# Layer 1's gate rows inside the attention's ring, key stacks of 48 rows, and transfers dealt to other queues

## The chip, the cores and the metric

The kernel runs on one core of a Trainium2 chip. The metric is the device time of one execution in microseconds (us), lower is better. Engines: TensorE (PE, its weight loads PEld), VectorE (DVE), ScalarE (ACT), GpSimd (POOL), and SyncE (SP), which only issues transfers; ScalarE issues transfers too, on a queue of its own.

## The reference

Two layers on 2 x 1024 tokens of 128 channels. Each layer computes an attention `s` and a feed-forward result `g` of the same normalised input; layer 1's feed-forward part has an expert-weighted attention of its own.

```python
def _layernorm(x, eps=1e-05): ...            # (x - mean) / sqrt(var + eps), per token
# x: 2 x 1024 tokens x 128
xn = _layernorm(x)                            # layer 0
s = _L0_attn_ref(xn, ...)                     # 16 heads of 8, bias by position, softmax over 1024 keys
g = _silu(_L0_ffn_ref(xn, ...))               # router, 8 experts of 256, 2 shared
x = x + s * g
xn = _layernorm(x)                            # layer 1
s = _L1_attn_ref(xn, W_Q, W_K, W_V, W_O)      # 16 heads of 8, causal softmax
g = _silu(_L1_ffn_ref(xn, ...))               # see below
x = x + s * g

def _gating(flat_hs, sim, gates, min_experts):
    logits = _normalize(flat_hs, -1) @ _normalize(sim, 0) - sigmoid(gates)
    ...                                       # relu, at least two experts kept, softmax over them

def _L1_ffn_ref(x, ...):
    n1 = _layernorm(x, ln1_w, ln1_b)
    rw = _gating(n1, smha_sim, smha_gates, 2)
    q = einsum('btc,ech,bte->bth', n1, q_proj, rw)   # k and v alike
    hs = x + (causal attention of q, k, v, put back by o_proj and rw)
    n2 = _layernorm(hs, ln2_w, ln2_b)
    rw2 = _gating(n2, moe_sim, moe_gates, 2)
    return hs + (8 experts w1, gelu, w2, weighted by rw2)
```

## The kernel before

Everything is written out by hand: each engine has one program, and semaphores join them. Layer 0's feed-forward part and its attention come first; then, in `attention(1)`, layer 1's attention; then layer 1's expert part, whose first expert units already run in the attention's last two halves.

**Halves and steps.** The heads of a batch are taken in groups of four (HG = 4). A group's 1024 queries are two halves, so there are 16 halves H (HALVES). For each half the kernel computes the transposed scores, key tile by key tile ("T steps": 4 in an even half, 8 in an odd one, with 512, 384, 256 and 128 queries in the last four), takes their exponentials on ScalarE (line 1090), and multiplies by the values one step later (`av_step`). The exponent needs each row's maximum. It comes from a second product of the same scores with the queries on the partitions ("S units", `ring_unit` and `both`), whose results pass through four PSUM banks, the ring; VectorE reduces each (line 1605). When all S units of a half are reduced, unit "K" combines them (line 1598), GpSimd splits the maxima in three bf16 parts (`max_parts`, lines 916 to 919), unit "M" transposes the parts on TensorE, VectorE copies them to `mrow` (line 1610), and SP's `max_rows` (line 689) puts them as rows 48 to 50 under the half's query stack with four transfers. TensorE starts half H after all of them have landed (`pe.wait_ge(A["m_ld"], 64 * (H + 1))`). The key stack has ones in rows 48 to 50, so one product of 51 rows subtracts the maximum. These ones stand in DRAM with the keys, and `load_group` fetches 51 rows (TROWS) of keys and 48 (ROWS) of queries per piece.

**The order.** `s_stream` gives the order of units; `stands_before` puts 16 S units of half 0, K and M of half 0, and 14 S units of half 1 ahead of the first half; `even_steps` deals the rest to the T steps: (8, 8, 8, 10) S units to the four steps of half 0, four to every later step until none are left. TensorE issues an S unit right behind each T product. VectorE follows the same order.

**Around layer 1's start.** Before the 16 first S units VectorE does `normal_again(1)` (line 1379) and `batch_values(1)` (line 1741) for the second batch. TensorE transposes `zz` in four chunks; ScalarE makes `n1T` and its square. Behind the 14 S units, `gate_rows` (lines 1835, 1888) computes the gate logits and sums of squares in banks 4 to 6; ScalarE copies the rows (line 1050), VectorE the logits (`gate_raw`, lines 1486 to 1488), ScalarE takes a root (line 1118) and then loads its table for the exponential.

**SP's loop.** For half H: `sums_out(H - 1)` (line 693) fetches the softmax sums; `sums_back(H - 1)` stores their inverse (line 699) and loads it back spread (line 704); `max_rows(H + 2)`; then what the table `then` says: in 9 to 13 the gate weights as rows spread over 128 partitions (`rw_behind`, line 819, 1 MB each). VectorE's `invert(H - 1)` (line 1620) waits for the sums behind step 3 of an even half and step 4 of an odd one. ScalarE issues the loads of the next key and query stacks, and of projection weights, at the start of halves 1 to 9 (lines 601, 604).

Of the kernel before, what the change touches and what calls it, by code (L numbers as in the profile page):

```python
# [33 lines left out]
P = 128  # L34
# [136 lines left out]
def even_steps(stream, first):  # L171
# [116 lines left out]
def block_net(nc, a, out):  # L288
    ctx = ExitStack()
    with ctx:  # L290
# [11 lines left out]
        k_dram = [dram(f"k_dram{l}", (GROUPS * HG, TROWS, SEQ), BF16) for l in range(2)]  # L302
# [76 lines left out]
        ones_rows = bf(62, 2)[0:32 * PARTS, :]  # L379
# [212 lines left out]
        def load_group(eng, l, G, pieces=range(4)):  # L592


            for piece in pieces:
                hh = piece // 2
                dr, rows, at_ = ((q_dram[l], ROWS, q_at[l]), (k_dram[l], TROWS, k_at[l]))[piece % 2]
                src = bass.AP(tensor=dr.tensor, offset=(G * HG + hh) * rows * SEQ,
                              ap=[[SEQ, rows], [2 * rows * SEQ, PAIRS], [1, SEQ]])
                dst = bf(at_[G], 4)[64 * hh:64 * hh + rows, :].rearrange("p (r t) -> p r t", r=PAIRS)  # L600
                eng.dma_start(dst, src).then_inc(att[l][f"ld{G // 2}"], 16)

# [4 lines left out]
        def store_qk(eng, l, b):  # L607
# [15 lines left out]
            for row, parts in K_ROWS:  # L623
                for n in range(parts):
                    dst = bass.AP(tensor=k_dram[l].tensor, offset=(b * HEADS * TROWS + (row + n) * HD) * SEQ,
                                  ap=[[TROWS * SEQ, HEADS], [SEQ, HD], [1, SEQ]])
# [7 lines left out]
        def _(sp):  # L634
# [45 lines left out]
            def max_rows(l, H):  # L680

                A, G, h = att[l], H // 2, H % 2
                sp.wait_ge(A["ring_free"], place[l]["M", H] + 1)
                if H:
                    sp.wait_ge(A["m_ld"], 64 * H)
                for j in range(HG):
                    row, first = 64 * (j % 2) + ROWS, 12 * (PAIRS * (j % 2) + j // 2)
                    dst = Qs[l][G][row:row + PARTS, j // 2, 512 * h:512 * (h + 1)].rearrange("p (q t) -> p q t", t=P)
                    sp.dma_start(dst, mrow[first:first + 12, H % 2, :]).then_inc(A["m_ld"], 16)  # L689
# [16 lines left out]
            def attention_feed(l, then):  # L706
# [4 lines left out]
                store_qk(sp, 1, 1)  # L711
                max_rows(l, 1)
# [66 lines left out]
            for l in range(2):  # L779
# [1674 lines left out]
```

## Time and profile before

| | us |
|---|---|
| median of 3 runs | 1192.28 (1189.81 to 1196.51) |
| the profiled execution | 1190.6, of which its span is 1188.8 |
| busy in the span: PE, DVE, ACT, POOL | 1063.3, 811.4, 646.5, 210.0 |
| layer 1's attention, first S unit to its last M | about 639 to 897 |
| mean granted TensorE clock | 0.941 of full speed |

Times in the rows are us from the span's start. The page gives for each engine the busy time and its share; a timeline row gives start, duration, engine, line, operation, "output<-input", a count where alike instructions are merged, and in brackets how long the engine had been idle and what released it.

### The profile page before, as it was taken

To read this page: it belongs to the slowest core of one execution; us is meant where nothing else is said; L and a number is where in the kernel's file an instruction comes from. 1 tells how busy PE (TensorE), PEld (TensorE's weight loads), DVE (VectorE), ACT (ScalarE), POOL (GpSimd) and SP (SyncE) were. 2 spreads that over 40 slices of the span, in tenths; PEclk is the share of its full clock that TensorE was granted. 3 is DMA by queue.
4 is the path that set the end of the run, shared out by engine and by line. 5 is a ranking of instruction groups with operands and counts; after the bars stand their busy time and mean duration, and the time that the engine had idled before them with its cause. 6 is when DMAs were issued, how large, how long until landed. Compare 5 with 4: busy or idle time off the path is not lost.

```text
span 1188.8 us, 19388 instructions
## 1 busy us (share of the span) xinstructions
PE 1063.3 (89%) x7308; PEld 490.5 (41%) x7308; DVE 811.4 (68%) x1625; ACT 646.5 (54%) x1259; POOL 210.0 (18%) x327
## 2 busy tenths in 40 slices
PE   5699999999999999999977888899889999888767
PEld 4455555552222222222234333334334468543444
DVE  7656666667887888875377778888674156655654
ACT  4522222226898888889733366677565432442534
POOL 2244554510010101010003011113221000001100
PEclk9899999999999999999976799899898999999888
DMA  4684112001010111000023422211322020000431
GB/s 128 201 229 140 50 66 81 2 1 28 25 43 30 43 30 34 12 20 20 11 66 97 151 66 75 60 45 42 126 86 88 10 80 1 1 1 0 143 143 36
DMA packets 57398, 74.63 MB, mean 63 GB/s; under 512 B 15720, under 2 KB 35032, under 8 KB 55512
## 3 DMA queue, kind: packets, MB, share of 16 engines
q1 hardware_dynamic: 48516, 62.13, 16.5%
q10 hardware_dynamic: 8788, 11.26, 3.4%
q8 instruction: 58, 0.95, 0.3%
q14 instruction: 36, 0.29, 0.1%
HBM read 58.18 MB, written 14.54 MB: 61 GB/s over the span
## 4 chain that ended last, share of the span: by engine, by line
PE 69%; DVE 19%; ACT 6%; issue 3%; DMA 2%; SPq 1%; ACTq 0%; POOL 0%; DVEq 0%
PE PS L1835 67%; DVE mx L1605 9%; ACT arena L1090 4%; DMA sums<-arena 1%; PE PS L1848 1%; DVE arena L1809 1%; DVE arena L1404 1%; DVE arena L1379 1%; DVE arena L1364 0%; DVE arena L1407 0%; DVE small L1795 0%; SPq L689 0%; DMA arena<-in_L_attn_x 0%; PE PS L2307 0%; DVE fw L1700 0%
## 5 line engine op out<-in xcount | busy, mean ns | idle before, releaser
L1835 PE MATMUL PS<-arena 128*32 128x512 f32 (+10 forms) x3656 | 568.1, 479 | 50.3 <-DVE mx L1605 22.8
L1605 DVE TENSOR_REDUCE mx<-PS 128x1 f32<-128x512 f32 (+3 forms) x896 | 511.9, 625 | 88.7 <-PE PS L1835 86.8
L1090 ACT ACTIVATE arena<-PS 128x512 f32<-128x512 f32 (+3 forms) x896 | 435.3, 558 | 149.3 <-PE PS L1835 145.0
L1835 PEld LDWEIGHTS PS<-arena 128*32 128x32 f32 (+3 forms) x3656 | 149.1, 104 | 409.5 <-ACT arena L1090 183.6
L1835 PE MATMUL PS<-x_hi,w_hi_lo 128*128 128x512 f32 x320 | 145.7, 496 | 6.8 <-ACT fw L1133 2.3
L1133 ACT ACTIVATE fw<-PS 128x512 f32<-128x512 f32 x80 | 47.8, 598 | 168.0 <-PE PS L1835 168.0
L1700 DVE TENSOR_TENSOR fw<-PS,fw 128x512 f32<-128x512 f32 x80 | 55.3, 692 | 79.2 <-PE PS L1835 76.6
L1835 PE MATMUL PS<-fw 128*128 128x512 f32 (+3 forms) x184 | 98.4, 620 | 0.0
L1001 POOL TENSOR_TENSOR fw<-fw,arena 128x512 f32<-128x512 f32 x64 | 81.8, 1280 | 76.1 <-DVE fw L1700 76.1
L925 POOL TENSOR_TENSOR arena<-arena,fw 128x512 f32<-128x512 f32 x31 | 39.4, 1272 | 262.8 <-DMA fw<-sum_dram 262.8
L1835 PEld LDWEIGHTS PS<-x_hi,w_hi_lo 128*128 128x128 f32 x320 | 61.5, 192 | 37.8 <-issue 21.2
L1835 PE MATMUL PS<-arena,fw 128*128 128x512 f32 x128 | 66.1, 635 | 5.2 <-DVE arena L1791 5.2
L1835 PE MATMUL PS<-x_lo,w_hi_lo 128*128 128x512 f32 x160 | 63.8, 399 | 0.0
L1835 PE MATMUL PS<-identb_sw,mask_kq_sw 64*128 64x128 bf16 x256 | 55.2, 230 | 0.0
L1835 PE MATMUL PS<-identb,mask_kq 64*128 64x128 bf16 x256 | 54.4, 229 | 0.0
L1835 PE MATMUL PS<-mask_kq,identb 64*128 64x128 bf16 x256 | 53.5, 223 | 0.0
L1835 PE MATMUL PS<-mask_kq_sw,identb_sw 64*128 64x128 bf16 x256 | 53.4, 223 | 0.0
L916 POOL CAST mparts<-mneg 128x16 bf16<-128x16 f32 x24 | 4.7, 196 | 260.0 <-DVE mneg L1598 260.0
L1835 PE MATMUL PS<-e_hi_lo,w_hi_lo 128*128 128x512 f32 x144 | 45.3, 395 | 0.0
L1835 PE MATMUL PS<-e_hi_lo,fw_lo 128*128 128x512 f32 x104 | 41.5, 400 | 0.0
L1821 DVE TENSOR_TENSOR arena<-arena 128x512 f32<-128x512 f32 x32 | 21.9, 697 | 26.3 <-ACT arena L1321 26.3
L1835 PEld LDWEIGHTS PS<-x_lo,w_hi_lo 128*128 128x128 f32 x160 | 30.9, 193 | 21.6 <-issue 17.9
(317 smaller groups left out, 1110.1 us busy)
## 6 DMA issues: line engine op xcount, KB each, us to landing
arena<-comb_dram SPq DMA_DIRECT2D x14, 1024.0 KB, 4.8
arena<-comb_dram SPq DMA_DIRECT2D x18, 512.0 KB, 7.4
fw<-sum_dram SPq DMA_DIRECT2D x31, 256.0 KB
q_dram<-arena SPq DMA_DIRECT2D x24, 256.0 KB, 3.7
k_dram<-arena SPq DMA_DIRECT2D x24, 256.0 KB, 4.0
arena<-k_dram ACTq DMA_DIRECT2D x20, 204.0 KB
arena<-q_dram ACTq DMA_DIRECT2D x20, 192.0 KB
arena<-drev_dram SPq DMA_DIRECT2D x16, 192.0 KB, 6.9
```

Source lines behind the costliest of these rows:

```text
L925: g.tensor_tensor(OT[:, G, 512 * h:512 * (h + 1)], Osb[:, h, :], RB[l][:, h, :], ALU.mult).then_inc(A["r_done"], 1)
L1001: g.tensor_tensor(fu[:, k % 4, :], fu[:, k % 4, :], cwb[:, (e - 1) % 2, chunk(part_of(k))], ALU.mult).then_inc(g_made, 1)
L1090: s.activation(Pr[:, m % 8, 0:w], st_bank(l, m, 0, w), ACT.Exp).then_inc(A["e_done"], 1)
L1133: s.activation(ft[:, k % 2, :], bank(2), ACT.Silu).then_inc(a_made, 1)
L1379: ins = v.tensor_scalar(dst[:, t, :], src[:, t, :], small[:, 0, t:t + 1], small[:, 2, t:t + 1], ALU.subtract, ALU.mult)
L1404: v.tensor_tensor(src, src, dst[:, 0, :], ALU.subtract).then_inc(rest_done, 1)
L1605: v.reduce_max(mx[:, H % 2, kh, n:n + 1], bank(ring_bank[l][U], 0, w), axis=AX.X, negate=True).then_inc(A["ring_free"], 1)
L1700: v.tensor_tensor(fu[:, k % 4, :], bank(3), ft[:, k % 2, :], ALU.mult).then_inc(u_made, 1)
L1809: v.tensor_tensor(Xo[:, x % 4, :], attnT[:, chunk(n)], rwb[e][:, chunk(n)], ALU.mult).then_inc(ox_made, 1)
L1821: v.tensor_tensor(gg[:, U % 4, :], ga[:, U % 4, :], rwb[e][:, chunk(2 * b + c)], ALU.mult).then_inc(i_g, 1)
L1835: return nc.tensor.matmul(out_, lhsT, rhs, start=start, stop=stop)
L1848: ins = nc.tensor.transpose(bank(first + c, P * k, P * (k + 1)), src(4 * c + k), ident[:, :])
```

## The change

Five things. **Gate rows**: the gate's row product is now a ring unit "R" behind step 1 of half 0 and the transposes with the squares' sum a ring unit "L" behind step 2; VectorE copies both out (the row copy was ScalarE's); the root moves to ScalarE's half 2, step 2, and a one-column exponential is put where it stood. Half 0's steps take (6, 8, 8, 8) S units, four fewer, so that every later unit comes one step later, and the last four S units with K and M of half 15 fall in half 14. **Key stacks**: keys are stored and loaded with 48 rows; the ones go once to `ones_dram` and from there under the stacks, by two transfers at the start and two behind `store_qk(1, 1)`. **First rows**: half 0's four row transfers are issued by SP (two) and ScalarE (two); ScalarE loads group 2 before the `n1T` activations. **Values behind first maxima**: VectorE does `normal_again(1)` behind the first 16 reductions and `batch_values(1)` behind the first `mrow` copy; TensorE transposes two chunks of `zz` before M of half 0 and two behind it. **Weight rows**: the 1 MB weight rows are issued by ScalarE at the start of halves 10 to 13, where SP issued them in loops 9 to 13.

```diff
@@ even_steps: where the score units go
-            count = HG if H else (8, 8, 8, 10)[i]
+            count = HG if H else (6, 8, 8, 8)[i]
...
+        if H == 0:
+            here[1].append(("R",))
+            here[2].append(("L",))
@@ DRAM and ones
-        k_dram = [dram(f"k_dram{l}", (GROUPS * HG, TROWS, SEQ), BF16) for l in range(2)]
+        k_dram = [dram(f"k_dram{l}", (GROUPS * HG, ROWS, SEQ), BF16) for l in range(2)]
+        ones_dram = dram("ones_dram", (8 * PARTS, SEQ), BF16)
...
-        ones_rows = bf(62, 2)[0:32 * PARTS, :]
+        ones_rows = bf(62, 2)[0:8 * PARTS, :]
@@ load_group
-                dr, rows, at_ = ((q_dram[l], ROWS, q_at[l]), (k_dram[l], TROWS, k_at[l]))[piece % 2]
+                dr, at_ = ((q_dram[l], q_at[l]), (k_dram[l], k_at[l]))[piece % 2]
...
+        def send_rows(eng, l, H, heads):
+            A, G, h = att[l], H // 2, H % 2
+            eng.wait_ge(A["ring_free"], place[l]["M", H] + 1)
+            if H:
+                eng.wait_ge(A["m_ld"], 64 * H)
+            for j in heads:
...
+                eng.dma_start(dst, mrow[first:first + 12, H % 2, :]).then_inc(A["m_ld"], 16)
@@ SP
             def max_rows(l, H):
...
+                send_rows(sp, l, H, range(2) if l == 1 and H == 0 else range(HG))
...
                 max_rows(l, 0)
                 store_qk(sp, 1, 1)
+                sp.wait_ge(z_ready, 12)
+                ones_under(32)
                 max_rows(l, 1)
...
-            for l in range(2):
-                dst = bass.AP(tensor=k_dram[l].tensor, offset=ROWS * SEQ, ap=[[TROWS * SEQ, GROUPS * HG], [SEQ, PARTS], [1, SEQ]])
-                sp.dma_start(dst, ones_rows).then_inc(ones_stored, 16)
+            sp.dma_start(ones_dram, ones_rows).then_inc(ones_stored, 16)
+            sp.wait_ge(ones_stored, 16)
+            def ones_under(kib):
+                for hh in range(2):
+                    row = 64 * hh + ROWS
+                    dst = bf(kib, 16)[row:row + PARTS, :].rearrange("p (n t) -> p n t", t=SEQ)
+                    sp.dma_start(dst, ones_dram.rearrange("(p n) t -> p n t", p=PARTS)).then_inc(ones_stored, 16)
+            ones_under(48)
...
-            attention_feed(1, {
-                8: comb_out, 9: lambda: rw_behind(7, 0, 4), 10: lambda: rw_behind(7, 1), 11: lambda: rw_behind(7, 5),
-                12: lambda: rw_behind(11, 2), 13: lambda: rw_behind(11, 3)})
+            attention_feed(1, {8: comb_out})
@@ ScalarE
+                        if l == 1 and H == 2 and i == 2:
+                            root_squares(1)
...
-            act.wait_ge(ones_stored, 16 * 2)
...
+            first_batch()
             for c in range(NC):
                 act.wait_ge(tr_ps, 16 + c + 1)
                 s.activation(n1T[:, 512 * c:512 * (c + 1)], ...).then_inc(tr_ev, 1)
+                if c == 1:
+                    send_rows(act, 1, 0, range(2, HG))
             act.wait_ge(tr_ev, 20)
             s.activation(zz..., n1T[:, :], ACT.Square).then_inc(sq_ready, 1)
-            rows_out(1, 4)
-            root_squares(1)
+            s.activation(gl[:, 1, 159:160], ones[:, 0:1], ACT.Exp)
...
-                -1: first_batch, 1: lambda: next_group(1, 3), 2: later_batch,
+                1: lambda: next_group(1, 3), 2: later_batch,
...
-                HALVES - 2: last_rows})
+                10: lambda: rw_behind(7, 0, 4), 11: lambda: rw_behind(7, 1, 5), 12: lambda: rw_behind(11, 2),
+                13: lambda: rw_behind(11, 3), HALVES - 2: last_rows})
@@ VectorE
-                    sequence(first_units[l])
-                    gate_raw(1)
+                    sequence(first_units[l][:AHEAD])
+                    normal_again(1)
+                    sequence(first_units[l][AHEAD:AHEAD + 2])
+                    batch_values(1)
+                    sequence(first_units[l][AHEAD + 2:])
...
             queries(1)
-            normal_again(1)
-            batch_values(1)
             invert_sums = attention(1)
@@ TensorE
+                    transposes(lambda t: zz[:, t, :], 4, lambda c: pe.wait_ge(z_ready, 7 + c), (0, 1))
+                    for what in first_units[l][AHEAD:AHEAD + 2]:
+                        ring_unit(what)
                     pe.wait_ge(v_ev, 8)
-                    transposes(lambda t: zz[:, t, :], 4, lambda c: pe.wait_ge(z_ready, (7, 8, 11, 12)[c]))
-                    for what in first_units[l][AHEAD:]:
+                    transposes(lambda t: zz[:, t, :], 4, lambda c: pe.wait_ge(z_ready, 9 + c), (2, 3))
+                    for what in first_units[l][AHEAD + 2:]:
                         ring_unit(what)
                     pe.wait_ge(tr_ev, 20)
-                    gate_rows(1, n1T, 4, 6)
-                    pe.wait_ge(ss_ready, 1)
```

VectorE at the start of layer 1's attention, before (mx: maxima, mrow: row copy, gl: gate logits):

```order
L1734 TENSOR_SCALAR arena<-PS 128x512 x2
L1377 RECIPROCAL small<-small 128x8
L1379 TENSOR_SCALAR arena<-arena,small 128x128 x8
L1741 COPY arena<-PS 128x4x4x32 x2
L1605 TENSOR_REDUCE mx<-PS 128x1 x16
L1610 CAST mrow<-PS 48x128
L1605 TENSOR_REDUCE mx<-PS 128x1 x14
L1486 COPY gl<-PS 128x128
L1487 COPY gl<-PS 128x16
L1488 COPY gl<-PS 128x8
```

and in the changed kernel:

```order
L1757 TENSOR_SCALAR arena<-PS 128x512 x2
L1621 TENSOR_REDUCE mx<-PS 128x1 x16
L1394 RECIPROCAL small<-small 128x8
L1396 TENSOR_SCALAR arena<-arena,small 128x128 x8
L1626 CAST mrow<-PS 48x128
L1764 COPY arena<-PS 128x4x4x32 x2
L1621 TENSOR_REDUCE mx<-PS 128x1 x28
L1628 COPY arena<-PS 128x512
L1621 TENSOR_REDUCE mx<-PS 128x1 x5
L1614 TENSOR_TENSOR mneg<-mx 128x16
```

The first 16 reductions now stand ahead of the second batch's normalisation, and the gate copies are gone from behind the 14.

VectorE between the `mrow` copy of half 3 and the inversion of half 1's sums, in half 2, before:

```order
L1598 TENSOR_TENSOR mneg<-mx 128x16
L1605 TENSOR_REDUCE mx<-PS 128x1 x4
L1610 CAST mrow<-PS 48x128
L1605 TENSOR_REDUCE mx<-PS 128x1 x11
L1620 RECIPROCAL rsums<-sums 128x16
```

and in the changed kernel:

```order
L1614 TENSOR_TENSOR mneg<-mx 128x16
L1621 TENSOR_REDUCE mx<-PS 128x1 x4
L1626 CAST mrow<-PS 48x128
L1621 TENSOR_REDUCE mx<-PS 128x1 x7
L1640 RECIPROCAL rsums<-sums 128x16
```

Seven units instead of eleven lie between the copy and the end of the even half; halves 4, 6, 8, 10 and 12 read alike.

## Rows read from the trace of the kernel before

**Rows 1.** The page: the chain that ended last, shares of the span.
```profile
PE 69%; DVE 19%; ACT 6%; issue 3%; DMA 2%; SPq 1%; ACTq 0%; POOL 0%; DVEq 0%
```
**Rows 2.** Timeline of VectorE, layer 1's start.
```profile
636.12 2.14 DVE L1379 TENSOR_SCALAR arena<-arena,small 128x128 f32<-128x128 f32 x8
...
639.39 6.65 DVE L1605 TENSOR_REDUCE mx<-PS 128x1 f32<-128x384 f32 x16
649.01 0.28 DVE L1610 CAST mrow<-PS 48x128 bf16<-48x128 f32 x1 [2.97 <-PE PS L1835]
649.33 6.53 DVE L1605 TENSOR_REDUCE mx<-PS 128x1 f32<-128x512 f32 x14
659.70 0.29 DVE L1486 COPY gl<-PS 128x128 f32<-128x128 f32 x1 [3.83 <-PE PS L1888]
...
660.77 3.61 DVE L1605 TENSOR_REDUCE mx<-PS 128x1 f32<-128x256 f32 x7 [0.63 <-PE PS L1835]
```
**Rows 3.** Timeline of TensorE: zz's transposes, gate rows, half 0, first product of half 1.
```profile
645.19 3.61 PE L1848 MATMUL PS<-ident,arena 128*128 128x128 f32 x16
...
654.59 1.95 PE L1835 MATMUL PS<-n1T,router 128*32 128x512 f32 x8
656.30 1.96 PE L1835 MATMUL PS<-arena,sum_col 128*32 128x512 f32 x8
...
664.61 0.39 PE L1835 MATMUL PS<-arena 51*128 51x512 bf16 x2 [1.98 <-ACT arena L1090]
...
679.60 3.01 PE L1835 MATMUL PS<-arena 51*128 51x512 bf16 x18 [0.63 <-DMA arena<-mrow]
```
**Rows 4.** Timeline of ScalarE: the table load before the first exponentials.
```profile
662.66 1.28 ACT L1090 ACT_TABLE_LOAD   x1 [2.26 <-issue]
```
**Rows 5.** Timeline of VectorE: row copies of halves 1 and 11, waits for sums.
```profile
675.14 0.27 DVE L1610 CAST mrow<-PS 48x128 bf16<-48x128 f32 x1
...
831.15 0.27 DVE L1610 CAST mrow<-PS 48x128 bf16<-48x128 f32 x1
...
841.78 0.25 DVE L1620 RECIPROCAL rsums<-sums 128x16 f32<-128x16 f32 x1 [4.71 <-DMA sums<-arena]
...
874.11 0.25 DVE L1620 RECIPROCAL rsums<-sums 128x16 f32<-128x16 f32 x1 [2.16 <-DMA sums<-arena]
```
**Rows 6.** Timeline of TensorE: M of half 11, steps 2, 3, half 11 starts.
```profile
830.42 0.24 PE L1835 MATMUL PS<-identb,mparts 128*48 128x128 bf16 x1 [0.70 <-POOL mparts L919]
...
834.63 0.32 PE L1835 MATMUL PS<-arena 51*128 51x128 bf16 x2
...
836.45 2.00 PE L1835 MATMUL PS<-arena 51*128 51x512 bf16 x16
...
842.64 0.28 PE L1835 MATMUL PS<-arena 48*128 48x128 bf16 x1 [4.19 <-DVE mx L1605]
```
**Rows 7.** Timeline of SP's queue: issues, with how long each took.
```profile
710.35 0.35 SPq L699 DMA_DIRECT2D sum_dram<-rsums  x1
717.60 0.57 SPq L704 DMA_DIRECT2D fw<-sum_dram  x1
...
831.45 3.04 SPq L689 DMA_DIRECT2D arena<-mrow  x4
834.54 1.75 SPq L819 DMA_DIRECT2D arena<-comb_dram  x2
836.33 0.62 SPq L693 DMA_DIRECT2D sums<-arena  x1
842.06 0.31 SPq L699 DMA_DIRECT2D sum_dram<-rsums  x1
843.47 0.58 SPq L704 DMA_DIRECT2D fw<-sum_dram  x1
```
**Rows 8.** Waits over the whole run: TensorE for key stacks (us, times, longest).
```profile
PEld PS L1835 <- DMA arena<-k_dram: 1.7, 3, 0.8
```
**Rows 9.** Transfers from 678.9 to 686 in 40 slices: share of 16 engines, tenths.
```profile
DMA  0000029839966995413212121121211212121122
```

More of the change, by code:

```diff
@@ L624, in store_qk @@
                 for n in range(parts):
-                    dst = bass.AP(tensor=k_dram[l].tensor, offset=(b * HEADS * TROWS + (row + n) * HD) * SEQ,
-                                  ap=[[TROWS * SEQ, HEADS], [SEQ, HD], [1, SEQ]])
+                    dst = bass.AP(tensor=k_dram[l].tensor, offset=(b * HEADS * ROWS + (row + n) * HD) * SEQ,
+                                  ap=[[ROWS * SEQ, HEADS], [SEQ, HD], [1, SEQ]])
                     src = kspb[b][:, n, :] if l else ksp[:, n, b * SEQ:(b + 1) * SEQ]
@@ L680, in max_rows @@
             def max_rows(l, H):
[L682 to L689, printed above, removed]
+                send_rows(sp, l, H, range(2) if l == 1 and H == 0 else range(HG))
             def sums_out(l, H):
@@ L789, in _ @@
             load_up(2)
-            sp.wait_ge(ones_stored, 16 * 2)
             sp.wait_ge(qk_stored[0][0], 16 * 12)
@@ L814, in _ @@
             assert rw_at[6:] == (24, 40)
-            def load_rw(n, *experts):
-                for e in experts:
-                    sp.dma_start(rwb[e], rows[n][e].partition_broadcast(P)).then_inc(rw_in[e], 16)
             def comb_out():
@@ L1185, in _, with first_batch @@
                 split_hi(1, b)
+            def first_batch():
+                act.wait_ge(qk_stored[1][0], 16 * 12)
+                next_group(1, 2)
+            first_batch()
             for c in range(NC):
@@ L1203, in later_batch, with rw_behind @@
                 proj_weights(act, 0, "q_proj")
+            def rw_behind(H, *experts):
+                act.wait_ge(comb_stored, 32)
+                act.wait_ge(att[1]["st_ps"], HG * steps_before(1, H + 1))
+                rows = comb_dram[1].rearrange("(e t) k -> e (t k)", e=EXP)
+                for e in experts:
+                    act.dma_start(rwb[e], rows[e].partition_broadcast(P)).then_inc(rw_in[e], 16)
             def last_rows():
@@ L1610, in sequence @@
                             v.tensor_copy(mrow[:, H % 2, :], bank(ring_bank[l][U], 0, P)[0:48, :]).then_inc(A["ring_free"], 1)
+                        elif what[0] == "R":
+                            v.tensor_copy(lrow[1], bank(ring_bank[l][U])).then_inc(A["ring_free"], 1)
+                        elif what[0] == "L":
+                            gate_raw(ring_bank[l][U], A["ring_free"])
                         else:
@@ L1948, in ring_unit @@
                         pe.wait_ge(A["mp_ready"], what[1] + 1)
+                    elif what[0] == "R":
+                        pe.wait_ge(tr_ev, 20)
+                        pe.wait_ge(sq_ready, 1)
+                    elif what[0] == "L":
+                        pe.wait_ge(A["ring_free"], place[l]["R",] + 1)
+                        pe.wait_ge(setup_done, 2)
                     else:
@@ L1973, in ring_unit @@
                         mm(bank(ring_bank[l][U], 0, P)[0:48, :], mparts[:, what[1] % 2, :], identb[:, :]).then_inc(A["ring_full"], 1)
+                    elif what[0] == "R":
+                        squares = zz.rearrange("p t c -> p (t c)")
+                        for c in range(NC):
+                            dst = bank(ring_bank[l][U])[32 * c:32 * (c + 1), :]
+                            mm(dst, router[:, 1, :], n1T[:, chunk(c)], stop=False)
+                            ins = mm(dst, sum_col[:, :], squares[:, chunk(c)], start=False)
+                        ins.then_inc(A["ring_full"], 1)
+                    elif what[0] == "L":
+                        for k in range(4):
+                            nc.tensor.transpose(bank(ring_bank[l][U], P * k, P * (k + 1)), lrow[1][:, P * k:P * (k + 1)], ident[:, :])
+                        mm(bank(ring_bank[l][U], 16, 16 + EXP), ones[:, :], simsq[:, 0, :]).then_inc(A["ring_full"], 1)
                     else:
```

26 lines of the change are left out of this document (12 added, 14 removed).

## The prediction

> **What bounds the kernel now.** I read the chain that ended last first: TensorE holds 69% of it and VectorE 19% [rows 1], and the table of times has TensorE busy for 1063.3 of 1188.8 us. So a change of order pays only where TensorE now stands still, and costs wherever it makes TensorE stand. Then I read the timelines of layer 1's attention for such places. There are four. At its start VectorE goes idle 2.97 us before the first `mrow` copy and 3.83 us before the gate copies, and 0.63 us after them [rows 2]. In half 0 TensorE waits 1.98 us for the first exponentials [rows 3], behind a 1.28 us table load on ScalarE [rows 4]. VectorE waits 4.71 us in half 10 and 2.16 us in half 12 for softmax sums [rows 5], and TensorE stands still 4.19 us with it [rows 6]. For key stacks TensorE waits 1.7 us in the whole run [rows 8]. The change goes at all four. I make the sum against the profiled execution's own 1190.6 us, which lies 1.7 below the median of 1192.28. A measurement of this kernel tells about 0.5%, 6 us, from no change: "faster" is below 1186.3, "slower" above 1198.2.
>
> **1. From the start to half 1: -0.7.** Before, the 16 first reductions wait for the normalisation (2.14 from 636.12) and the value copies, start at 639.39 and end 6.65 later at 646.0 [rows 2]. Now they start with their products, of which the first are there by about 639.1, so they gain only 0.3. Then comes what stood ahead: the normalisation, 2.1, to 648.0, then the `mrow` copy, not earlier than 648.2 (649.01 before), then the values, 1.1, to 649.7. TensorE must wait for these before the last eight transposes, half of the 16 that took 3.61 [rows 3], 1.8 us. So VectorE starts the rest at about 652.1, and 14 reductions at 6.53 per 14 [rows 2] are done at 658.6. Before, the reductions of half 0's steps began at 660.77; now they follow at once, 2.2 earlier, because the gate rows and the copies behind them are gone. The 1.98 us wait for ScalarE [rows 3] came from the table load [rows 4], now done beforehand; of it I count 0.8, since a first exponential has to be made before TensorE's second group in any case. That is -3.0. Against it: unit R on TensorE lasts from 654.59 to 658.26, 3.67 us [rows 3], in one block in half 0; the ring's four banks feed VectorE for about 2 of them, so 1.7 is lost. VectorE's own work in half 0 is four reductions less (3.61 for seven [rows 2], about 0.4 each, so -1.5) and the row copy (0.6, as ScalarE's) and the gate copies (0.5) more: -0.4. And half 1's rows: only 7 units at 0.47 (6.53 / 14) follow the `mrow` copy in half 0 instead of 11. Before, TensorE could go on 4.46 us after the copy, and waited 0.63 of it [rows 3, 5]; now the 7 units fill 3.3, no more than 2.8 of it surely under TensorE's work, and the wait is about 1.6: +1.0. Together -3.0 + 1.7 - 0.4 + 1.0 = -0.7. Bounds: -5 if R lies under the exponentials, +2 if the clock makes R and the transposes slower.
>
> **2. The root in half 2: +1.0.** Its two table loads at 1.28 [rows 4] and the root stop ScalarE for 2.8 us, in step 2. Three score buffers cover most of it, and part overlaps the wait of item 3. Bounds 0 and +2.8.
>
> **3. The rows of odd halves: +6.6.** This is what the four units fewer cost. Each later unit is one step later, so M of an odd half now stands in step 2 of the even half ahead of it, not in step 1, as the order shows by 7 units instead of 11 behind the copy. Nothing before shows an odd half waiting, since there was a step to spare: the `mrow` copy of half 11 is at 831.15 [rows 5], TensorE begins half 11 at 836.45 [rows 6], 5.30 later. One step less, and the last step took 1.82 (834.63 to 836.45 [rows 6]), leaves 3.5. The rows cannot be there by then: SP issues four transfers in 3.04 from 0.30 behind the copy [rows 7], so the last goes out 3.34 behind it, and in half 1 TensorE could go on 4.46 behind it [rows 3, 5]. The wait is 0.7 to 1.4, I take 1.1; halves 3, 5, 7, 9, 11, 13 pay: 6 x 1.1 = +6.6. Bounds: 0, if TensorE comes no sooner than the rows because VectorE sets its pace in these steps, and 6 x 1.4 = +8.4.
>
> **4. Weight rows on ScalarE's queue: -6.4.** In loop 10 SP issues the rows of half 11, then two 1 MB loads (1.75), and only then the sums (836.33) [rows 7]. VectorE's waits for them, 4.71 and 2.16 [rows 5], go if the sums go out right behind the row transfers, 3.4 behind the copy. I leave 0.5 for what is late next, the next `mrow` copy. The bounds are -6.9 and 0. The two 1 MB loads themselves end as before: nothing needs them until the expert part.
>
> **5. Key loads of 48 rows: -1.3.** TensorE's 1.7 us for key stacks [rows 8] go. The load ahead of half 1 ends in a tail of one to two tenths of the 16 engines for about 5 us [rows 9]: few engines carry it, and the others stay free for rows and sums. I take three quarters of the 1.7; bounds -1.7 and 0. The Trainium skill, "DMA: Bandwidth & Descriptors", "Why a DMA increments its semaphore by 16 and not by 1", says that a transfer runs on the largest number of engines up to 16 that divides the slowest dimension of both sides: 51 rows on 3, 48 on 16. The tail in the trace agrees with 3 of 16. By that rule the wait for keys would go wholly, -1.7 and not -1.3, but the keys would then stand on all 16 engines in the way of rows and sums, which speaks for rival C. The ones' transfers at the kernel's start lie under SP's other waits, those for group 4 and up lie between the store and half 1's rows, 15 us later; without that cover each costs an issue of about half a us.
>
> **6. The end: +0.8.** The last four S units, K and M of half 15 move into half 14's first step, whose expert work leaves VectorE busy; M then comes about one step (1.8) later. Bounds 0 and +2.7.
>
> **7. Shared transfer engines: +1.0.** ScalarE's loads at the start of odd halves now go out when the last row transfer and the sums are under way. At a clean place SP's two sum transfers are 1.41 apart (842.06, 843.47); with a stack's loads in flight they were 7.25 apart (710.35, 717.60) [rows 7]. Behind 2 MB the sums took from 834.54 to 841.78 [rows 5, 7]. Bounds 0 and +15 (four halves at up to 3.8). On this the Trainium skill, "DMA: Bandwidth & Descriptors", "Issuing engines are not separate DMA queues", speaks against item 4: it says that transfers of any engine run on the same 16 engines and that a second issuer saves only issue time. By it item 4 would save only the issues, 1.75 in half 10 and half of that in half 12, so -2.6 in place of -6.4, and the sum would be +4.8; carried further it is rival C.
>
> Sum: -0.7 + 1.0 + 6.6 - 6.4 - 1.3 + 0.8 + 1.0 = +1.0, so **1191.6**, 0.7 below the median of before. Everything else is nothing: the expert part and layer 0 are untouched, and pairs of steps hold the same widths as before, only in another pairing.
>
> **The rivals.** *A, the trade* (the forecast): 1191.6, no change that can be told. *B, the odd halves do not wait.* If VectorE sets TensorE's pace in steps 2 and 3, TensorE comes to the odd half later than 3.5 behind the copy. For it: VectorE stands in 19% of the chain [rows 1]; against it, TensorE's 69%. Then item 3 is +1, items 2 and 7 are 0 and item 1 is -3: 1190.6 - 3 + 1 - 6.4 - 1.3 + 0.8 = 1181.7. *C, slower: the sums collide with ScalarE's loads.* At the start of halves 3, 5, 11 and 13 a stack or 1 MB load goes out within a us of the sums. VectorE has only 7 units (3.3) and not 11 (5.1) before it needs them, so the lateness that was covered shows: sums are needed about 5.2 behind the copy and are issued at 3.4; each us beyond 1.8 of flight is paid. With 2 us in each of halves 3 and 5, 0.5 in 7 and 9, and item 4 given back in 11 and 13, it is 1191.6 - 1.0 + 4.0 + 1.0 + 6.4 = 1202. It decides from sums that land later than 5.2 behind the copy. For it: the 7.25; against it, a load of two pieces is small (0.4 MB beside the 2 MB) and the 2 MB alone took 7.2. *D, R makes half 0 TensorE's at a low clock*: +5 on A, 1196.6; for it R's 3.67 in one block.
>
> **How the numbers follow.** A 0.45, B 0.32, C 0.18, D 0.05. B is faster in 0.28 of 0.32, A in 0.06; slower are C's 0.17, A's 0.02 and D's 0.01. Faster 0.34, same 0.46, slower 0.20. The range reaches below B's 1181.7 by 2.7 for the pairing of steps and above C's 1202 by 1: 1179 to 1203.
>
> **What would show it.** Right: no wait over 0.5 for sums at the end of halves 10 and 12; at the start of halves 3 to 13 a wait of TensorE for the row transfers of 0.7 to 1.4; the first reduction at about 639.1, those of half 0 from about 658.6; four table loads near half 2 instead of none; no TensorE wait for keys. B: the waits for rows are missing, and TensorE reaches odd halves over 4.4 behind the copy. C: VectorE waits for sums over 1 us in halves 2, 4, 10 and 12. The forecast is wrong if the odd halves start on time, or if the sums stay late on their own queue.

## The result and the profile after

The changed kernel takes 1213.94 us (median of 4 runs, 1207.84 to 1216.48), the kernel before 1192.49 (4 runs): 1.017 of it, 95% interval [1.012, 1.022]. It is slower, by some 20 us, and lies outside the range. The profiled executions have spans of 1210.3 and 1188.8 us.

The page of the changed kernel, TensorE's busy row and the chain that ended last:

```profile
PE 1066.2 (88%) x7308; PEld 492.1 (41%) x7308; DVE 814.3 (67%) x1626; ACT 649.1 (54%) x1261; POOL 209.7 (17%) x327
...
PE 68%; DVE 18%; ACT 7%; issue 3%; DMA 2%; SPq 1%; ACTq 1%; POOL 0%; DVEq 0%
```

The span is 21.5 us longer, but TensorE is busy for 2.9 us more and no other engine for over 3; the chain is that of [rows 1] within a point. So most of the loss is waiting, and the chain's shares do not name it. ScalarE's copy of a half's output, once per half behind the next half's first step, cuts the run into stretches. Before:

```profile
600.44 0.60 ACT L1067 ACTIVATE arena<-PS 128x512 f32<-128x512 f32 x1 [2.06 <-PE PS L1835]
...
682.71 0.59 ACT L1067 ACTIVATE arena<-PS 128x512 f32<-128x512 f32 x1
...
899.02 0.59 ACT L1067 ACTIVATE arena<-PS 128x512 f32<-128x512 f32 x1
...
947.53 0.60 ACT L1067 ACTIVATE arena<-PS 128x512 f32<-128x512 f32 x1 [0.55 <-PE PS L1835]
```

and in the changed kernel (the four places, here and above, are the end of layer 0, first step of half 1, first step of half 14, and end of layer 1's attention):

```profile
603.26 0.60 ACT L1071 ACTIVATE arena<-PS 128x512 f32<-128x512 f32 x1 [2.06 <-PE PS L1856]
...
690.14 0.59 ACT L1071 ACTIVATE arena<-PS 128x512 f32<-128x512 f32 x1
...
915.05 0.63 ACT L1071 ACTIVATE arena<-PS 128x512 f32<-128x512 f32 x1
...
966.98 0.60 ACT L1071 ACTIVATE arena<-PS 128x512 f32<-128x512 f32 x1 [0.55 <-PE PS L1856]
```

The difference grows by 2.8 us in layer 0, 4.6 from there to half 1, 8.6 from half 1 to half 14, 3.4 in the last two halves and 2.1 behind them. The 2.1 are not explained: no edit lies there, and this last stretch takes between 241.2 and 246.3 us in the profiles of the runs below. The 8.6 are a net figure, since the kernel before lost 4.71 and 2.16 us to late sums in this stretch [rows 5].

The waits from 636 to 930 us, which is most of layer 1's attention (each line: who waits <- for what: us in all, times, longest), before and then in the changed kernel:

```profile
DVE rsums L1620 <- DMA sums<-arena: 7.6, 3, 4.7
PE PS L1835 <- DMA arena<-mrow: 0.6, 1, 0.6
```

```profile
DVE rsums L1640 <- DMA sums<-arena: 21.7, 5, 6.6
PE PS L1856 <- DMA arena<-mrow: 17.6, 6, 4.5
```

Both grew. VectorE's five waits stand at the ends of halves 4, 6, 8, 10 and 12, TensorE's six at the starts of halves 1, 5, 7, 9, 11 and 13. The turn from half 10 to half 11 shows both; VectorE, SP, ScalarE and TensorE of the changed kernel:

```profile
851.14 0.27 DVE L1626 CAST mrow<-PS 48x128 bf16<-48x128 f32 x1
851.33 2.46 DVE L1621 TENSOR_REDUCE mx<-PS 128x1 f32<-128x512 f32 x6
854.08 0.29 DVE L1621 TENSOR_REDUCE mx<-PS 128x1 f32<-128x128 f32 x1 [0.28 <-PE PS L1856]
860.95 0.25 DVE L1640 RECIPROCAL rsums<-sums 128x16 f32<-128x16 f32 x1 [6.58 <-DMA sums<-arena]
```

```profile
851.44 3.04 SPq L617 DMA_DIRECT2D arena<-mrow  x4
854.52 0.60 SPq L701 DMA_DIRECT2D sums<-arena  x1
```

```profile
854.11 0.81 ACTq L1219 DMA_DIRECT2D arena<-comb_dram  x2
```

```profile
858.54 0.60 PE L1856 MATMUL PS<-arena 51*128 51x512 bf16 x2 [4.53 <-DMA arena<-mrow]
```

The copy of the rows is at 851.14. VectorE is through its seven reductions at 854.37, 3.2 us behind it, and wants the sums. SP asks for them only at 854.52, since they stand on its queue behind the rows, and they come at 860.95. TensorE is ready for half 11 at 854.0 (4.53 before 858.54), 2.9 behind the copy. The rows land 7.4 behind it and not 4.46 [rows 3, 5], with 2 MB put on the way by ScalarE at 854.11; that these loads are the reason is what `u_late` and `u_rwsp` test. In halves 7, 9 and 11 ScalarE's loads go out 0.43, 0.43 and 0.37 us before SP has issued the last row transfer, and the rows land 6.0, 6.4 and 7.4 behind the copy; in halves 5 and 13 it is 0.33 and 0.24, and they land 4.5 behind it. So some tenths of a us may decide, but the loads of these halves also differ in size, and the two were not told apart.

### The profile page after: what moved, and what is told of

It reads as the page before. It is cut to its first block, busy times and chain, and to the rows that moved or that the text cites. A ratio compares the mean times of both kernels' runs of the same rounds, so it can differ in the third digit from the quotient of the medians.

```text
span 1210.3 us, 19406 instructions
## 1 busy us (share of the span) xinstructions
PE 1066.2 (88%) x7308; PEld 492.1 (41%) x7308; DVE 814.3 (67%) x1626; ACT 649.1 (54%) x1261; POOL 209.7 (17%) x327
## 4 chain that ended last, share of the span: by engine, by line
PE 68%; DVE 18%; ACT 7%; issue 3%; DMA 2%; SPq 1%; ACTq 1%; POOL 0%; DVEq 0%
PE PS L1856 66%; DVE mx L1621 8%; ACT arena L1094 4%; DMA arena<-mrow 1%; SPq L617 1%; DVE arena L1396 1%; PE PS L1869 1%; DMA sums<-arena 1%; DVE arena L1421 1%; DVE arena L1830 1%; PE PS L2349 0%; DVE arena L1381 0%; DVE arena L1424 0%; DVE small L1816 0%; DMA arena<-in_L_attn_x 0%
## 5 line engine op out<-in xcount | busy, mean ns | idle before, releaser
L1856 PE MATMUL PS<-arena 128*32 128x512 f32 (+12 forms) x3656 | 573.0, 482 | 63.7 <-DVE mx L1621 17.7
L1005 POOL TENSOR_TENSOR fw<-fw,arena 128x512 f32<-128x512 f32 x64 | 81.8, 1280 | 78.5 <-DVE fw L1723 78.5
```

The lines of the kernel that those rows point to most:

```text
L1005: g.tensor_tensor(fu[:, k % 4, :], fu[:, k % 4, :], cwb[:, (e - 1) % 2, chunk(part_of(k))], ALU.mult).then_inc(g_made, 1)
L1856: return nc.tensor.matmul(out_, lhsT, rhs, start=start, stop=stop)
```

## The experiments

Ratios are to the kernel before, with 95% intervals. The kernel before was measured again beside each group of runs, with medians from 1192.5 to 1195.7 us, so the ratios compare better than the times. Each run undoes or adds the part named in its edit: `u_` runs undo a part of the changed kernel, `b_` runs add one to the kernel before, `e_` runs put something new on the changed kernel, and `c_` and `s_` runs undo several parts.

| kernel | median, us | ratio |
|---|---|---|
| changed | 1213.9 | 1.017 [1.012, 1.022] |
| u_steps | 1193.4 | 1.0001 [0.9978, 1.0025] |
| u_keys | 1217.1 | 1.0184 [1.0141, 1.0227] |
| u_norm | 1209.7 | 1.0133 [1.0106, 1.016] |
| u_late | 1200.2 | 1.0056 [1.0029, 1.0083] |
| u_rwsp | 1216.7 | 1.0195 [1.0173, 1.0217] |
| b_steps | 1218.4 | 1.0207 [1.0181, 1.0233] |
| b_rwact | 1184.1 | 0.9925 [0.9907, 0.9944] |
| e_sums | 1201.6 | 1.0062 [1.0041, 1.0083] |
| e_sumslate | 1193.5 | 0.9991 [0.9971, 1.0011] |
| c_three | 1181.7 | 0.9908 [0.9887, 0.9928] |
| c_sums | 1182.2 | 0.9904 [0.9889, 0.9918] |
| c_sums_root | 1184.8 | 0.9929 [0.9911, 0.9947] |
| s_norm | 1187.3 | 0.993 [0.9903, 0.9957] |
| s_keys | 1188.8 | 0.9936 [0.991, 0.9961] |

### One step, undone and alone

```diff
 u_steps, on the changed kernel
-            count = HG if H else (6, 8, 8, 8)[i]
+            count = HG if H else (8, 8, 8, 10)[i]
 b_steps, on the kernel before
-            count = HG if H else (8, 8, 8, 10)[i]
+            count = HG if H else (6, 8, 8, 8)[i]
```

u_steps, expected: 

> The changed kernel with half 0's steps dealt (8, 8, 8, 10) score units again, all else kept. Theory 1 (one step less is the cause): the rows of odd halves go out one step earlier, so TensorE's six waits for them (1.5 to 4.5 us each, 17.6 in all) vanish, ScalarE's loads again go out behind the rows, and the sums of even halves come within 1 us of need: 11 to 14 us back, about 1200 to 1203. Theory 2 (ScalarE's loads collide with rows and sums wherever the rows stand): the sums waits of 3 to 6.6 us on VectorE stay and no more than 6 us come back, 1208.

b_steps, expected: 

> The kernel before with half 0's steps dealt (6, 8, 8, 8) score units and nothing else changed, so that all later units come one step later. Theory 1 (the one step is the cause by itself): TensorE waits for the rows in six odd halves, 1.5 to 4.5 us each, VectorE waits for the sums in the same halves, and the kernel takes 14 to 21 us more, 1207 to 1214. Theory 2 (it needs the other edits, ScalarE's 1 MB loads and 48-row loads above all): 5 to 8 us more, 1200.

Undone, the step gives back all 20 us; alone on the kernel before it costs 25. Both are more than either theory had. The waits in the same window, first u_steps, then b_steps:

```profile
DVE rsums L1640 <- DMA sums<-arena: 0.6, 1, 0.6
PE PS L1856 <- DMA arena<-mrow: 0.3, 1, 0.3
```

```profile
DVE rsums L1620 <- DMA sums<-arena: 39.4, 8, 7.6
PE PS L1835 <- DMA arena<-mrow: 16.8, 7, 3.3
```

In mechanism theory 1 holds in both: the waits go with the step and come with it. The kernel before stood at an edge. Its rows can land 4.46 us behind their copy [rows 3, 5] and half 11 began at 5.30 [rows 5, 6]; its sums can land some 5.2 behind the copy (worked out under item 7 below) and were needed at 5.9. Four score units fewer in half 0 pushed the rows over the edge at every odd half from 1 to 13 and the sums at every even one from 2 to 12.

Not all of b_steps's loss is waiting. From ScalarE's output copy in half 1 to that in half 14 it takes 236.3 us, before 216.3; of these 20.0, 7.2 are TensorE's busy time, 196.1 against 188.9 for the same 2132 products, at a mean granted clock of 0.85 against 0.92. The same stretch has 190.9 at 0.89 in the changed kernel and 185.1 at 0.94 in b_rwact. So the clock is a part of every difference in this stretch. That it falls because TensorE waits is likely from this order, but no run holds the one and changes the other.

### What the step costs with: sums behind rows, loads beside rows

```diff
 e_sums: SP's loop
-                    if H >= 1:
-                        sums_out(l, H - 1)
-                    if H >= 1:
-                        sums_back(l, H - 1)
-                    if H + LAG[l] < HALVES:
-                        max_rows(l, H + LAG[l])
+                    if H >= 1:
+                        sums_out(l, H - 1)
+                        if H + 1 < HALVES:
+                            max_rows(l, H + 1)
+                        sums_back(l, H - 1)
 u_late: ScalarE's transfers of odd halves of layer 1
-                    if H in loads:
+                    if H in loads and not (l == 1 and H % 2):
                         loads[H]()
...
+                        if l == 1 and H % 2 and i == 1 and H in loads:
+                            loads[H]()
```

u_late, expected: 

> The changed kernel with ScalarE's transfers of odd halves of layer 1 issued behind step 1 of the half and not at its start, all else kept. Theory 1 (they collide with the last row transfers and the sums): the rows land 4.5 us behind the row copy in every odd half, TensorE waits 1.5 at each and not up to 4.5, VectorE waits under 1.5 for sums: 8 to 11 us back, 1203 to 1206. Theory 2 (the rows are late by the step alone): under 3 us back, the waits of 3.1 to 4.5 in halves 7, 9, 11 stay.

e_sums, expected: 

> The changed kernel with SP asking for the sums of half H-1 ahead of the rows of half H+1 and not behind them, all else kept (the rows' transfers stand 0.6 us later). Theory 1 (half of the price is the sums, which stand on SP's queue behind rows that come a step later): VectorE's five waits for sums, 21.7 us, go, TensorE's waits for rows stay at about 18, and 6 to 10 us come back, 1204 to 1208. Theory 2 (the price is TensorE's wait for rows alone, and the sums' wait lies beside it): under 3 us back, 1211 or more.

e_sumslate (both edits), expected: 

> The changed kernel with both: sums ahead of rows on SP's queue, and ScalarE's transfers of odd halves behind step 1. Rows land 4.5 to 5 us behind the row copy, TensorE waits 1.5 to 2 us in six halves, no wait for sums. Theory 1 (rows late by one step cost 1.5 each, the rest was collisions and sums): 1196 to 1200, 3 to 5 above the kernel with the steps undone. Theory 2 (the two cures are of one cost): no better than the run with late loads alone, 1200.

The waits of u_late, e_sums and e_sumslate, in this order:

```profile
DVE rsums L1642 <- DMA sums<-arena: 10.3, 6, 2.1
PE PS L1858 <- DMA arena<-mrow: 9.5, 6, 1.8
```

```profile
PE PS L1855 <- DMA arena<-mrow: 15.7, 6, 3.5
```

```profile
PE PS L1857 <- DMA arena<-mrow: 9.5, 6, 1.8
```

Loads out of the way (u_late): 0.011 of the time back, 14 us, more than the 8 to 11 forecast. The rows now land early enough for waits of 1.5 to 1.8 at all six halves, so the loads were the reason for the longer ones. Sums first (e_sums): 0.011 as well, 12 to 13 us, and no wait for sums is left; more than the 6 to 10 expected. The profile puts 9.8 of it between halves 1 and 14. Another 1.7 lie between halves 2 and 6 of layer 0, where the edit also moves the rows ahead of the stored inverses; u_steps, without that edit, has 1.5 there, so this part can't be put down to the sums. Both (e_sumslate): 0.018, all that undoing the step gives.

Neither theory foresaw the last: TensorE still waits 9.5 us for rows, and yet the kernel is as fast as u_steps, which waits 0.3. TensorE's other waits in the same window say what the late step buys, first u_steps, then e_sumslate (`mparts` are the maxima that GpSimd splits in three):

```profile
PE PS L1856 <- ACT arena L1094: 11.6, 19, 2.2
PE PS L1856 <- POOL mparts L923: 5.0, 5, 2.7
PE PS L1856 <- DVE mx L1621: 5.0, 12, 1.7
```

```profile
PE PS L1857 <- ACT arena L1093: 6.5, 13, 2.2
PE PS L1857 <- DVE mx L1622: 4.0, 10, 1.5
PE PS L1857 <- POOL mparts L922: 2.8, 1, 2.8
```

Of 9.2 us more for the rows, 8.3 come back at GpSimd's maxima, ScalarE's exponentials and the ring. From the output copy in half 1 to that in half 14 e_sumslate takes 207.9 us and u_steps 213.1, with TensorE busy for 185.0 at a clock of 0.94 against 188.6 at 0.92. Behind the attention e_sumslate loses 2.6 again, which is not explained. A late step with sums first and loads late, on the parts of c_three below (209.6 in this stretch), was not tried.

### Weight rows

```diff
 b_rwact, on the kernel before
-                8: comb_out, 9: lambda: rw_behind(7, 0, 4), 10: lambda: rw_behind(7, 1), 11: lambda: rw_behind(7, 5),
-                12: lambda: rw_behind(11, 2), 13: lambda: rw_behind(11, 3)})
+            attention_feed(1, {8: comb_out})
...
+                10: lambda: rw_by_act(7, 0, 4), 11: lambda: rw_by_act(7, 1, 5), 12: lambda: rw_by_act(11, 2),
+                13: lambda: rw_by_act(11, 3), HALVES - 2: last_rows})
 u_rwsp: the reverse, on the changed kernel
```

b_rwact, expected: 

> The kernel before with the 1 MB weight rows issued by ScalarE at the start of halves 10 to 13 and nothing else changed. Theory 1 (they held SP's queue): VectorE's waits for sums of 4.7 and 2.2 us are gone, the stretch from half 9 to half 14 is 7 to 9 us shorter, 1184 to 1187. Theory 2 (they only share the transfer engines, so it doesn't matter who issues): waits of 2 to 4 us for sums or rows in the same halves, no more than 2.6 back, 1190.

u_rwsp, expected: 

> The changed kernel with the 1 MB weight rows back on SP's queue, all else kept. Theory 1 (ScalarE's 1 MB loads, issued before the last rows have landed, hold up the rows): TensorE's wait at half 11 falls from 4.5 to 1.5, but the sums stand behind the loads again, so halves 11 and 13 give back 2 to 4 us at most, 1210 to 1214. Theory 2 (on either queue the loads cost the same there): unchanged within 2 us, the wait for sums at half 11 over 6.

b_rwact's waits, then u_rwsp's:

```profile
DVE rsums L1626 <- DMA sums<-arena: 1.0, 2, 0.8
PEld PS L1841 <- DMA arena<-mrow: 0.2, 1, 0.2
```

```profile
DVE rsums L1646 <- DMA sums<-arena: 24.5, 6, 7.2
PE PS L1862 <- DMA arena<-mrow: 14.7, 6, 3.7
```

With the steps as before, this part alone is worth 0.0075, 9 us. The waits for sums fall by 6.6, which is item 4's 6.4; the stretch from half 1 to half 14 is 10.0 shorter, and 3.7 of it are TensorE's busy time at the higher clock. With the steps late the part is worth nothing that these runs can tell (1.0195 against 1.017), theory 2 of u_rwsp. On ScalarE's queue the 2 MB meet the rows and on SP's the sums: in u_rwsp half 11's wait for rows is 1.47 and not 4.53, and the wait for sums just ahead of it is 7.22 and not 6.58. Issuers are no lanes of their own, as the Trainium skill, "DMA: Bandwidth & Descriptors", "Issuing engines are not separate DMA queues", says, and the 7.4 us of half 11's rows agree. But the conclusion that I drew from it, 2.6 instead of 6.4, is refuted by b_rwact. What the move bought was not issue time alone: before, the 2 MB went out at 834.54, between the rows and the sums [rows 7], and in b_rwact they go out at 829.98, ahead of the rows (834.11) and 7.3 ahead of the sums (837.26). Whether the other queue or the earlier time does it was not told apart.

### Key stacks of 48 rows

```diff
 u_keys, on the changed kernel
-                dr, at_ = ((q_dram[l], q_at[l]), (k_dram[l], k_at[l]))[piece % 2]
+                dr, rows, at_ = ((q_dram[l], ROWS, q_at[l]), (k_dram[l], TROWS, k_at[l]))[piece % 2]
...
+                dst = bass.AP(tensor=k_dram[l].tensor, offset=ROWS * SEQ, ap=[[TROWS * SEQ, GROUPS * HG], [SEQ, PARTS], [1, SEQ]])
+                sp.dma_start(dst, ones_rows).then_inc(ones_stored, 16)
```

u_keys, expected: 

> The changed kernel with key stacks of 51 rows again, ones in DRAM, all else kept. Theory 1 (issues of 48-row key loads hold ScalarE): the issues of 1.34 and 1.48 us in layer 0 fall to 0.33 and layer 0 is 2.9 us shorter (its last row copy at 563.3, not 566.1), and in layer 1 the rows of halves 7, 9 land 1.5 us sooner: 4 to 6 us back, 1208 to 1210. Theory 2 (the 2.9 us are chance of the clock): layer 0 stays as it was or differs without a change in the issues' times, and under 2 us come back.

Theory 1 is right for layer 0 and wrong for the whole. ScalarE's issues at the start of layer 0's half 6, before and in the changed kernel:

```profile
394.20 0.31 ACTq L601 DMA_DIRECT2D arena<-q_dram  x1
394.54 0.33 ACTq L601 DMA_DIRECT2D arena<-k_dram  x1
394.97 2.06 ACT L1090 ACTIVATE arena<-PS 128x512 f32<-128x512 f32 x4 [0.18 <-PE PS L1835]
```

```profile
394.68 0.31 ACTq L605 DMA_DIRECT2D arena<-q_dram  x1
395.02 1.48 ACTq L605 DMA_DIRECT2D arena<-k_dram  x1
396.61 2.06 ACT L1094 ACTIVATE arena<-PS 128x512 f32<-128x512 f32 x4 [1.34 <-PE PS L1856]
```

In the changed kernel's layer 0 the issue of a 48-row load right behind the query load takes 0.45 to 1.48 us; that of a 51-row load takes 0.32 or 0.33 there in all eight kernels that have it. The exponentials wait behind it. From the copy of half 2's output to that of half 6's, layer 0 takes 78.5 us in every kernel with 51 rows (78.52 before; u_keys, b_steps, b_rwact, c_three, c_sums, c_sums_root and s_keys 78.50 to 78.53) and 80.0 to 81.8 in each of the eight with 48 (the changed one 81.79; u_steps 80.34; s_norm 80.45). In the changed kernel the four issues of this stretch take 2.4 us longer together, of its 3.3. So chance does not explain it. Yet u_keys isn't faster as a whole: in layer 1 VectorE waits 31.4 us for sums and not 21.7. That a 51-row load stays longer beside the late sums may be the reason; it was not tried by itself.

### The normalisation's place

```diff
 u_norm, on the changed kernel (VectorE; TensorE's transposes in one block again)
-                    sequence(first_units[l][:AHEAD])
-                    normal_again(1)
-                    sequence(first_units[l][AHEAD:AHEAD + 2])
-                    batch_values(1)
-                    sequence(first_units[l][AHEAD + 2:])
+                    normal_again(1)
+                    batch_values(1)
+                    sequence(first_units[l])
```

u_norm, expected: 

> The changed kernel with VectorE's second normalisation and values ahead of the 16 first reductions again. Theory 1 (GpSimd's 4.2 us of work slows VectorE's normalisation when they run together): the eight instructions take 2.1 us and not 5.8, and half 0's row copy comes 3 us earlier than in the changed kernel, 3 us back, 1211. Theory 2 (the normalisation is slow for a reason of its own place, or the row copy then waits for TensorE): less than 1 us back.

VectorE in the changed kernel, and GpSimd beside it:

```profile
642.26 6.65 DVE L1621 TENSOR_REDUCE mx<-PS 128x1 f32<-128x384 f32 x16 [3.58 <-PE PS L1856]
...
649.05 5.76 DVE L1396 TENSOR_SCALAR arena<-arena,small 128x128 f32<-128x128 f32 x8
654.74 0.27 DVE L1626 CAST mrow<-PS 48x128 bf16<-48x128 f32 x1
654.94 1.27 DVE L1764 COPY arena<-PS 128x512 f32<-128x512 f32 x2
658.81 3.37 DVE L1621 TENSOR_REDUCE mx<-PS 128x1 f32<-128x512 f32 x8 [2.60 <-PE PS L1856]
```

```profile
641.71 4.21 POOL L954 TENSOR_TENSOR arena<-arena 128x1024 f32<-128x1024 f32 x2 [18.40 <-ACT arena L1047]
...
650.00 4.23 POOL L958 TENSOR_TENSOR arena<-arena 128x1024 bf16<-128x1024 f32 x2
```

In u_norm the same eight instructions run before GpSimd starts:

```profile
638.90 2.14 DVE L1396 TENSOR_SCALAR arena<-arena,small 128x128 f32<-128x128 f32 x8
```

The normalisation takes 5.76 us beside GpSimd's 4.23 and 2.14 alone. The reductions are not slowed: one of 128x512 takes 0.68 us beside GpSimd's first pair and 0.68 later, where GpSimd is mostly idle. u_norm gives back about 0.004, 4 us, as theory 1 says, but the two intervals overlap; what is sure is the duration, and half 0's row copy 2.4 us earlier (652.39, changed 654.74). The Trainium skill, "SBUF — State Buffer", "Who interferes with whom", has a rule for it, that `tensor_scalar` can contend with GpSimd over a shared port and a reduction never does; the trace agrees with both halves of it.

### The parts that are left

c_three has the steps, the 51 rows and the normalisation as before, so what is left of the change is the gate rows in the ring, the first rows on two queues and the weight rows. s_norm is c_three with 48 rows, s_keys is c_three with the normalisation late. c_sums is c_three with e_sums's order, c_sums_root has the root in half 3:

```diff
 c_sums_root, on c_sums
-                        if l == 1 and H == 2 and i == 2:
+                        if l == 1 and H == 3 and i == 2:
                             root_squares(1)
```

c_three, expected: 

> The changed kernel with three parts undone: half 0's steps at (8, 8, 8, 10), key stacks of 51 rows, VectorE's normalisation ahead of the first reductions. What is left: gate rows in the ring, first rows on two queues, weight rows on ScalarE's queue. If the costs add up as the single runs show (layer 0 3 us back, start to half 1 about 3 below the kernel before, weight rows 7 to 9 below, root and its table loads 3 above): 1182 to 1186. If they don't add up (the key loads on 3 engines meet rows and sums in layer 1, as in the run with 51 rows alone): 1190 to 1195, with waits for sums over 2 us in halves 2 to 8.

c_sums, expected: 

> The kernel of c_three (three parts undone, 1181.7) with the sums ahead of the rows on SP's queue. There VectorE waits 0.4 us for sums and TensorE 0.8 for rows in all. Theory 1 (the queue's order matters only where something waits): the same within 2 us. Theory 2 (rows 0.6 us later): TensorE waits 0.5 us at the odd halves, 1183 to 1185.

c_sums_root, expected: 

> The kernel of c_sums with the root and its two table loads in half 3, step 2 (queries 512 wide, eight steps) and not in half 2, step 2. Theory 1 (2.8 us of ScalarE in an even half's short steps come through, 1.6 us between halves 2 and 3): the stretch from half 2 to half 4 is 1.5 us shorter. Theory 2 (ScalarE has no more slack in an odd half): the same or longer, since its four exponentials fill 2.06 of each 2.4 us step there.

s_norm, expected: 

> The changed kernel with the steps at (8, 8, 8, 10) and the normalisation ahead of the reductions, so that of c_three only the key stacks differ: 48 rows here, 51 there. Theory 1 (48 rows cost what layer 0 shows, 1.8 to 3.3 us, and nothing in layer 1 once no rows stand in the way): 1184 to 1186. Theory 2 (48-row loads also hold ScalarE in layer 1, as the issues of 1.2 and 2.0 us at halves 2 and 3 of u_steps): 1187 to 1190.

s_keys, expected: 

> The changed kernel with the steps at (8, 8, 8, 10) and key stacks of 51 rows; of c_three only the normalisation's place differs. Theory 1 (its place costs 5.8 against 2.1 us beside GpSimd and the values' later copy, 4 to 7 us to the start of half 1, and all of it stays): 1186 to 1189. Theory 2 (later waits take part of it up): 1183 to 1185.

c_three takes 1181.7, 0.9908 of the kernel before, just under the 1182 to 1186 at which the parts would add up. 48 rows cost 0.0022 there (s_norm) and the late normalisation 0.0028 (s_keys), 3 us each. Both intervals overlap that of c_three, so neither size is shown; for the key stacks the stretch of layer 0 makes the sign sure, for the normalisation its duration. The theories of s_norm and s_keys are not decided either: beside these two the kernel before took 1195.7 and beside c_three 1193.5. By its time s_norm (1187.3) is in the second theory's range and by its ratio (about 1185) in the first's; s_keys (1188.8) is in the first's and by its ratio (about 1186) at that range's lower end. The sums' order changes nothing where nothing waits (c_sums, theory 1). The root in half 3 is no better (c_sums_root, theory 2): 1184.8 against 1182.2, intervals overlapping, and in the profiles the stretch from half 2 to half 4 is 1.6 longer. c_three and c_sums are the best versions found, about 11 us faster than the kernel before.

## Why the prediction was wrong

**Bound and places**: right. The waits were where I looked, and those of the kernel before could be removed, as b_rwact and c_three show.

**The step that failed is item 7, with rival C's condition.** I wrote that VectorE needs the sums about 5.2 us behind the copy, and so priced the late sums and the collisions together at 1.0. The same sentence says 7 units (3.3). The trace has the sums needed 3.2 to 3.4 behind the copy, at the ends of all five halves where VectorE waits for them. Asked for at 3.4 and 1.85 or more on their way (at the end of the kernel before, SP asks at 948.15 and the inversion is at 950.00), they could not be there before 5.2 even on free engines. That is about 1.9 in each of five halves, 9.5 us, and e_sums is 9.8 shorter between halves 1 and 14. (Half 2 had no such wait; there the need came later, 5.4 behind the copy.) The numbers were all in the rows of before; I took the time at which the sums could land for the time at which they were needed, as it made the two meet. In the kernel before the need came 5.9 behind the copy (831.15; 841.78 less 4.71 [rows 5]). Item 7 also says that ScalarE's loads go out while the last row transfer is under way, but prices them for the sums alone: the rows' share is put at nothing. It makes the waits for rows 3.1, 3.5 and 4.5 in halves 7, 9 and 11, and u_late, which takes the loads away from rows and sums, gives 14 us back. Both cures together give back the whole 20.

**Item 3** (rows of odd halves, +6.6): the mechanism is right. The clean size was 1.5 at each, not 1.1, just past its bound of 1.4: TensorE comes 2.9 to 3.0 behind the copy, earlier than the 3.1 that this bound stands for, and the rows land at 4.5 at best. Half 3, which was counted, did not wait. The price was left without its gain: with M a step later TensorE waits less for GpSimd's maxima, ScalarE and the ring, 8.3 us in e_sumslate against u_steps, so the row waits at their clean size cost nothing that the times show.

**Item 1** (-0.7): +4.6. The normalisation was costed at 2.1 from a place where GpSimd was idle and moved to one where it wasn't (3.6 more), and half 1's rows were 3.5 late and not 1.6, again by ScalarE's loads (1.8 in u_late). The first reductions gained nothing: they start at 642.26, and with 2.8 for layer 0 taken off that is 639.4 and not 639.1. With the place undone the stretch to half 1 is 3.3 shorter than before in u_norm and 2.4 in c_three, which agrees with the part of item 1 on gate rows and table load. **Item 2** (+1.0): 1.6, from half 2 to half 3 in c_three. **Item 4** (-6.4): right in its mechanism and for the waits (6.6 less in b_rwact), but the time gained, 9, lies past its bound of 6.9, and with the late steps u_rwsp shows nothing left of it. The loads that it names are issued in loop 9, not 10; nothing hangs on that. **Item 5** (-1.3): wrong sign. The wait of TensorE for keys did go, but I left out what issuing them costs ScalarE, and that made layer 0 longer, which the sum had at nothing. **Item 6** (+0.8): the last two halves took 3.4 more, past its bound; b_steps has 1.1 there and e_sumslate 1.7, and the rest is not explained.

**Rivals.** C was the right kind and had 0.18; its 1202 lacked the clean 9.5 us, the collision with the rows, and the losses of items 1 and 5. B failed: TensorE reached the odd halves early, as item 3 said. D can't be the cause: u_steps keeps unit R in half 0 and gives the whole 20 us back.

## What to carry to other kernels

When an order is shifted by one step, write for every transfer the time from its cause to its need, before and after, and price the difference: where a transfer takes 5.2 us from the copy ahead of it, a need at 5.9 that becomes one at 3.3 is a wait, however the total work stands. On a queue that waits in order, ask what stands behind the thing that has become late; here putting the sums ahead of the rows took away every wait for them, some 10 to 12 us. Ask also which waits the shift removes, since here they paid for the late rows. And take a moved instruction's duration from its new neighbours, not from its old place.

## What the runs showed of the hardware

- Issuing a load is not a fixed price for the engine that issues it. In layer 0 a key load of 51 rows behind a query load took 0.32 or 0.33 us to issue in eight kernels, one of 48 rows 0.45 to 1.48 in the changed kernel, with ScalarE's work standing behind it.
- Eight `tensor_scalar` instructions on 128x128 took 5.76 us beside GpSimd and 2.14 without it; a reduction of 128x512 from PSUM took 0.68 beside it and, on average, later.
- Four row transfers that land 4.5 us behind their copy when nothing else goes out took 7.4 with 2 MB issued by another engine 0.37 us before the last of them was out, and 6.0 and 6.4 with a key and a query load at 0.43. With other loads, at 0.33 and 0.24, they took 4.5.
- For the same 2132 products TensorE was busy 185.0 us at a mean granted clock of 0.94 (e_sumslate), 188.9 at 0.92 (before), 190.9 at 0.89 (changed) and 196.1 at 0.85 (b_steps).
